# Second attention of a four-layer kernel: values duplicated by GpSimd and q arranged earlier at its beginning; the last network's first two steps moved into its block at its end

## What is computed

```python
x = x + _layernorm(_L0_attn_ref(_layernorm(x), ...))   # linear attention, 16 heads of 128
x = x + _layernorm(_L0_ffn_ref(_layernorm(x), ...))    # 16 experts, top 2, and a shared network
x = x + _layernorm(_L1_attn_ref(_layernorm(x), ...))   # attention in windows of 32 tokens
x = x + _layernorm(_L1_ffn_ref(_layernorm(x), ...))    # SwiGLU network, 1024 wide

def _L1_attn_ref(x, Wq, bq, Wk, bk, Wv, bv, Wo, bo):   # WINDOW 32, 16 heads of 16, 2 groups
    starts = jnp.arange(num_windows) * (W // 2)
    scores = jnp.einsum('brgnqd,bgnkd->brgnqk', qg, kw) * scale
    attn = jax.nn.softmax(scores, axis=-1)
    og = jnp.einsum('brgnqk,bgnkd->brgnqd', attn, vw)
    o = og....reshape(B, num_windows * W, H * D)[:, :L, :]
    return o @ Wo + bo

def _L1_ffn_ref(h_shard, w_gate_up, w_down):
    gate, up = jnp.split(jnp.einsum('bsh,oh->bso', h_shard, w_gate_up), 2, axis=-1)
    h = jax.nn.silu(gate) * up
    return jnp.einsum('bsi,hi->bsh', h, w_down)
```

## Time and profile before

| | us |
|---|---|
| median of 3 runs | 1158.51 (1154.85 to 1162.67) |
| profiled execution, its own time | 1155.04 |
| its span in the trace | 1153.2 |

### The profile page before, as it was taken

How to read it: one execution, slowest core, us unless ns; L and a number is a source line. 1 busy time by engine, 2 the same in 40 slices (tenths; PEclk the granted TensorE clock), 3 DMA queues, 4 the chain that set the end, 5 groups by cost and what they waited for, 6 DMA issues and landing times. The chain is left out here.

```text
span 1153.2 us, 20280 instructions
## 1 busy us (share of the span) xinstructions
PE 1114.8 (97%) x7188; PEld 960.1 (83%) x7188; DVE 743.3 (64%) x1582; ACT 525.1 (46%) x978; POOL 252.7 (22%) x290
## 2 busy tenths in 40 slices
PE   8999999999999999999999999899998889899997
PEld 7997988989989989988988888775555778788897
DVE  6665665665665665665665677755554767686556
ACT  5675344344344344344344354555552466644322
POOL 1112021021021021111111131323332556323211
PEclk9999999999999999999999999799998969999999
DMA  4001001001001001001000000853333324000001
GB/s 156 11 1 37 11 1 38 9 0 36 9 0 36 9 0 36 9 0 36 9 0 1 1 1 4 318 123 97 98 102 96 87 77 147 1 1 1 19 19 38
DMA packets 27979, 48.28 MB, mean 42 GB/s; under 512 B 4780, under 2 KB 18060, under 8 KB 26764
## 3 DMA queue, kind: packets, MB, share of 16 engines
q1 hardware_dynamic: 23980, 37.62, 10.2%
q0 software_dynamic: 3456, 9.44, 3.1%
q10 hardware_dynamic: 480, 0.40, 0.1%
HBM read 35.65 MB, written 9.44 MB: 39 GB/s over the span
## 5 line engine op out<-in xcount | busy, mean ns | idle before, releaser
L880 POOL TENSOR_TENSOR linear_out_row<-linear_out_row,lin_sq 128x512 f32<-128x512 f32 x62 | 89.9, 1450 | 538.3 <-ACT lin_sq L745 536.0
L43 PE MATMUL lin_bank<-keep_xT_hi,lin_w_hi 128*128 128x512 f32 x382 | 154.2, 404 | 0.0
L44 PE MATMUL lin_bank<-keep_xT_lo,lin_w_hi 128*128 128x512 f32 x382 | 151.1, 395 | 0.0
L45 PE MATMUL lin_bank<-keep_xT_hi,lin_w_lo 128*128 128x512 f32 x382 | 150.8, 395 | 0.0
L825 DVE TENSOR_TENSOR lin_st<-lin_bank,lin_mask 128x512 f32<-128x512 f32 x64 | 44.0, 691 | 160.9 <-PE lin_bank L622 160.9
L741 ACT ACTIVATE lin_o<-lin_bank 128x512 f32<-128x512 f32 x64 | 38.3, 599 | 187.7 <-PE lin_bank L653 187.7
L649 PE MATMUL lin_bank<-lin_st,lin_v 128*128 128x128 f32 x512 | 93.8, 275 | 0.0
L653 PE MATMUL lin_bank<-lin_qd,lin_state 128*128 128x128 f32 x448 | 87.2, 276 | 0.0
L45 PEld LDWEIGHTS lin_bank<-keep_xT_hi,lin_w_lo 128*128 128x128 f32 x382 | 71.8, 188 | 17.5
L44 PEld LDWEIGHTS lin_bank<-keep_xT_lo,lin_w_hi 128*128 128x128 f32 x382 | 72.0, 189 | 14.6
L43 PEld LDWEIGHTS lin_bank<-keep_xT_hi,lin_w_hi 128*128 128x128 f32 x382 | 72.0, 188 | 14.6
(11 more groups left out here) (417 smaller groups left out, 2843.2 us busy)
## 6 DMA issues: line engine op xcount, KB each, us to landing
lin_raw<-in_wp SPq DMA_DIRECT2D x7, 1024.0 KB, 4.7
experts_up_expert_up<-in_wgu SPq DMA_DIRECT2D x16, 352.0 KB, 7.3
sorted_y<-shared_loaded SPq DMA_DIRECT2D x40, 128.0 KB, 1.7
linear_out_row<-in_wdn SPq DMA_DIRECT2D x4, 704.0 KB
lin_raw_out<-in_wop SPq DMA_DIRECT2D x8, 256.0 KB, 2.6
tokens_x<-linear_out_row SPq DMA_DIRECT2D x4, 512.0 KB, 10.3
linear_out_row<-in_ffn_up SPq DMA_DIRECT2D x2, 1024.0 KB, 5.8
tail_q<-tail_qT SPq DMA_DIRECT2D x28, 64.0 KB, 2.0
```

The source lines that it names most:

```text
L43: nc.tensor.matmul(out, lh, rh, start=first, stop=False, skip_group_check=skip)
L44: nc.tensor.matmul(out, lh, rl, start=False, stop=False, skip_group_check=skip)
L45: return nc.tensor.matmul(out, ll, rh, start=False, stop=last, skip_group_check=skip)
L880: pool.tensor_tensor(part, part, sq[:, a, :], ALU.add).then_inc(squares_sb, 1)
```

## The change

In `window_attention`, at the beginning: the value copies of batch 0 leave ScalarE; GpSimd makes them (four `tensor_copy`) after its tenth tile has arrived and ahead of b's scale. ScalarE issues half of the q moves of rr = 1 too, and does all four arrangements of batch 0 ahead of the loop (before, one was VectorE's in round 0 and one ScalarE's in round 2). TensorE turns b's tiles in round 2, behind the scores of job 2, instead of round 1.

At the end: `before` and `turn` for segment 0 each move to earlier rounds on GpSimd, VectorE and ScalarE; TensorE's turn goes from round 21 to round 18. Steps 0 and 1 of the last network's `pe_up` are issued in rounds 19 and 21, the split of the up weights of steps 0 to 2 in rounds 11 to 22. The statistics of segment 1 (`before`) move into round 20. In `feed_forward` the steps start with what is left of them, and weights are split three steps ahead, behind a step instead of in front of it. For this the banks, four semaphores, q2, q3 and the up weights are allocated in the scope "window" around both blocks (so `tail_bank` and `ffn_bank` are both called `window_bank`, and `ffn_w_hi` is `window_up_hi`).

```diff
@@ feed_forward
             def _(dve):
                 chain = Chain(dve, own)
                 dve.wait_ge(keep.ffn_ready, 1)
-                net.dve_low(dve, 0)
-                for half in range(2):
-                    before.statistics(dve, chain, 1, half)
-                net.dve_low(dve, 1)
+                net.dve_low_down(dve, 0)
                 for g in range(SEGS):
                     late = LATE if g == 0 else 0
                     for j in range(J):
-                        if g == 0 and j + 2 < J:
-                            net.dve_low(dve, j + 2)
                         net.dve_step(dve, chain, g, j)
+                        if g == 0 and j < 2:
+                            net.dve_low_down(dve, j + 1)
+                        if g == 0 and j + 3 < J:
+                            net.dve_low(dve, j + 3)
...
             def _(act):
                 act.wait_ge(keep.ffn_ready, 1)
-                net.act_high(act, 0)
-                net.act_high(act, 1)
+                net.act_high_down(act, 0)
...
                     for j in range(J):
-                        net.pe_up(pe, g, j)
+                        if g or j >= 2:
+                            net.pe_up(pe, g, j)
...
@@ window_attention, SP and GpSimd
-                        move_q(sp, b, rr, (0, 1) if b == rr == 0 else range(4))
+                        move_q(sp, b, rr, range(4) if b else (0, 1))
...
                     if n == BATCH * USED_TILES:
+                        for t_ahead in ORDER[n - AHEAD:n]:
+                            pool.wait_ge(arrived[t_ahead], 2 * DMA)
+                        pool.wait_ge(kv_sb, 2)
+                        for half in range(2):
+                            v = kvT[GD:2 * GD, 0, half * STEP:half * STEP + WPAIRS * WIN].rearrange("p (m k) -> p m k", k=WIN)
+                            for g in range(WG):
+                                pool.tensor_copy(vdup[GD:2 * GD, :, half, g, :], v).then_inc(vdup_sb, 1)
+                        pool.wait_ge(vdup_sb, 2 * WG)
                         b.pool_scale(pool, chain, "y")
                         b.pool_scale(pool, chain, "x")
...
                     if n == 6:
+                        before.affine.scale_and_shift(pool, chain, 0)
+                    if n == 7:
                         b.pool_shift_x(pool)
...
-                    if n == 7:
-                        before.affine.scale_and_shift(pool, chain, 0)
-                    if n == 11:
+                    if n == 10:
                         turn.affine.scale_and_shift(pool, chain, 0)
@@ window_attention, VectorE
-                    if i == NJ - 1:
+                    if i == NJ - 3:
                         dve.wait_ge(a.shifted, a.n)
                         before.add(dve, 0)
+                    if i == NJ - 2:
                         dve.wait_ge(before.added, 1)
                         for half in range(2):
                             turn.statistics(dve, chain, 0, half)
-                    if i == 0:
-                        arrange(0, 1)
...
-                    if i == NJ + 5:
+                    if i == NJ - 1:
+                        dve.wait_ge(s_mm, NJ)
+                        ffn.dve_low_up(dve, 0)
+                    if i == NJ + 1:
+                        ffn.dve_low_up(dve, 1)
+                    if i == NJ + 3:
                         turn.dve_low(dve, 0)
+                    if i == NJ + 4:
+                        for half in range(2):
+                            before.statistics(dve, chain, 1, half)
+                    if i == NJ + 6:
+                        ffn.dve_low_up(dve, 2)
@@ window_attention, ScalarE
                 take_q(0, 1)
-                duplicate(0)
-                arrange(0, 0)
+                move_q(act, 0, 1, (2, 3))
                 act.wait_ge(powered, 1)
                 act.activation(table[:], power[:, 0:1], ACT.Exp)
+                arrange(0, 0)
                 values(0)
-                arrange(1, 0)
+                for part in range(2):
+                    arrange(1, part)
+                arrange(0, 1)
...
-                    if i == 2:
-                        arrange(1, 1)
...
-                    if i == NB + 5:
+                    if i == NB + 3:
                         before.act_apply(act, 0)
+                    if i == NB + 4:
+                        for n in range(BATCH * RR):
+                            act.wait_ge(q3_sb[n], 2)
+                        ffn.act_high_up(act, 0)
+                    if i in (NB + 5, NB + 6):
+                        ffn.act_high_up(act, i - NB - 4)
...
-                    if i == NJ + 1:
+                    if i == NJ:
                         turn.act_apply(act, 0)
-                turn.act_high(act, 0)
+                    if i == NJ + 2:
+                        turn.act_high(act, 0)
@@ window_attention, TensorE
-                    if i == 1:
+                    if i == 2:
                         pe.wait_ge(used[0].low, KT + 1)
                         used[1].pe_turn(pe, turned)
...
-                    if i == NJ + 5:
+                    if i == NJ + 2:
                         turn.pe_turn(pe, 0)
...
+                    if i == NJ + 3:
+                        pe.wait_ge(less_sb, NJ)
+                        pe.wait_ge(pT_sb, NJ)
+                        pe.wait_ge(turn.low, KT)
+                        ffn.pe_up(pe, 0, 0)
+                    if i == NJ + 5:
+                        ffn.pe_up(pe, 0, 1)
```

84 lines of the change are left out of this document (56 added, 28 removed).

## The result

The changed kernel's median is 1162.49 us (1160.27 to 1173.19, 20 runs), that of the kernel before, run beside it, 1158.42 (1154.85 to 1162.67, 20 runs): a ratio of 1.0054 with an interval of 1.0037 to 1.0071. Forecast were 1157 and a change of -0.1%. The kernel became slower by half a per cent. That is inside the range of 1151 to 1163, and inside the 1% that was called no change.

A forecast was written before the change was run, and what follows sets the result against it. TensorE was taken as the bound, so only its standstills or lower clock matter. Terms -1.2, -1.5 and +1.4 sum to -1.3 us on the profiled 1155.04: 1153.7, or about 1157 as median; range 1151 to 1163.

The forecast's parts named there:

- +1.4 for the end: Segment 1's turn in the last network was to come later by 1.4 us, bounds +0.3 and +3.4.
- -1.3: Sum of all terms in us: -1.2 for job 3's sooner scores, -1.5 for the clock, +1.4 for the end.
- the 3.0 us by which the copies were to hold up VectorE: At the beginning, GpSimd's four copies, served between VectorE's sums of b, were to delay the first subtraction to 930.8.
- the clock's term: Full clock some 4 us earlier than at 945, speeding batch 1's values and projections: -1.5 us, bounds 0 and -3.
- The rival of copies that disturb nobody: At the beginning, copies quick or without disturbance: -3.5 to -4.8 in sum, 1154.5 us; chance 0.24.
- ScalarE's list: Ahead of the loop: DMA issues end at 923.8, arrangements at 931.0; nothing won on ScalarE there.
- 1.2 was summed: At the beginning, job 3's scores at 937.7 instead of 938.88, a gain of 1.2 us.
- The rival that the clock would return only with the projections: At the beginning, scores and turns would not bring full clock back earlier: +0.2 in sum, 1158.7 us; chance 0.20.
- -2.7 of the sum: The whole gain at the beginning: -1.2 for job 3's scores and -1.5 for the clock.
- The gap: At the change of blocks, TensorE waits 2.85 us, as step 2 needs step 0's product; step 2 starts at 1012.4.
- The rival "late turn": In the last block, TensorE stands over 3 us ahead of segment 1's turn, then lower clock: 1160.9 us; chance 0.18.
- The 1.65 us of lower clock at the change of blocks: TensorE's loss to a clock of 0.50 from 1007 to 1010 us, expected again in the changed kernel.

The follow-up runs named there:

- group 4: Runs of start_again, the changed end alone, and batch 1's sooner arrangement with and without the changed beginning; kernel before 1156.74 us, stops in 4 of 4 profiles.
- start_only: The kernel before with the edits of the beginning alone: 1159.53 us, ratio 1.0027 to the kernel before.
- start_again: The kernel before with the beginning of the change alone, run a second time, beside stops: 1159.55 us, ratio 1.0016.
- repeat: The changed kernel again, nothing left out, beside stops: 1160.92 us, ratio 1.0035 to the kernel before.
- groups 1, 4: Kernels run on one chip beside the kernel before, which took 1157.34 and 1156.74 us; ScalarE stops of 6 us or more in 4 of 4 profiles each.
- 2, 3 and 5: The other groups of runs; kernel before 1153.77, 1153.67 and 1154.03 us, with no ScalarE stop of 6 us or more in any profile.
- changed_third: The changed kernel a third time, nothing left out, where nothing stops: 1155.87 us, ratio 1.0010 to the kernel before.
- both: Changed kernel with batch 1's first arrangement behind round 7's subtraction, turn statistics ahead of splits, and ScalarE's `before` norm behind step 1's silu: 1150.66 us, ratio 0.9972.
- before_again: The kernel before, unchanged, run for a second profile, which has no stops: 1154.39 us, ratio 1.0002.
- arrange_b1: The changed kernel with VectorE's first arrangement of batch 1's q directly behind the subtraction of round 7: 1151.13 us, ratio 0.9978 to the kernel before.
- start_third: The kernel before with the beginning of the change alone, a third time, without stops: 1152.14 us, ratio 0.9984.

## Why the prediction was off, step by step

**On record.** Two costs add up to the +0.54%. The change's own are +0.1%: the beginning at 0.9984 and the whole at 1.0010 leave +0.26% or 3.0 us for the end, a difference between two groups, and the traces have 2.6. The rest, 0.4% or some 5 us, appears only beside stops. That stops cost the new beginning more than the old is shown by every profile that has them (the table in group 4). Up to the turn of segment 1 they leave the old beginning 0.8 to 1.4 us later than without them (three profiles), the new one 1.5 to 13.9 (start_only, start_again, repeat and the result's). That they make up the whole of the rest is argued, from groups 1, 4 and the result against 2, 3 and 5. What causes the stops is open: they came in two groups with every kernel, with either form of the beginning, and in the three others with none. The prediction had only one profile of the kernel before and no step for them. The measured 1162.49 lies inside the stated range by luck: its upper end was reckoned for a turn 3.4 us late with a second stretch of lower clock, and what brought the time there were mostly stops.

**Which steps failed.** The sum has nothing for the work behind batch 1's first projections, where 4.5 us of the beginning's gain are lost again, and it takes +1.4 for the end where 2.6 to 2.7 came. Together these turn -1.3 into +1.3. A third step, the 3.0 us by which the copies were to hold up VectorE, failed the other way, and so did the size of the clock's term up to job 8.

**GpSimd's copies: sized within bounds, their effect wrong.** The four copies, GpSimd's, and VectorE beside them in changed_third:

```profile
919.04 3.01 POOL L2572 COPY tail_oP<-linear_out_row 32x512 f32<-32x512 f32 x4 [2.04 <-DMA linear_out_row<-sorted_y,keep_slots]
920.31 0.71 DVE L2623 SCALAR_TENSOR_TENSOR keep_y<-linear_out_row,keep_weight,keep_y 128x256 f32<-128x256 f32 x1
927.94 0.68 DVE L2659 TENSOR_REDUCE tail_most<-window_bank 128x16 f32<-128x512 f32 x1
```

The four take 3.01 us together, 0.75 each from start to start (0.95 taken, 0.45 to 1.45 bounded). The failed step is "If each copy is served between two of them, VectorE is late by ... 3.0". The worst of VectorE's sums beside a copy takes 0.71 instead of 0.48, and the first subtraction begins at 927.94 where the earlier trace rows have 927.78: late by 0.2 and not 3.0 (0.3 counted from batch 0's projection, 0.5 to 0.6 in the other profiles without stops). The Trainium skill's page "SBUF — State Buffer", section "Who interferes with whom", calls the port pair that the two engines share an exclusive lock. The rows agree that they disturb each other: the single copies take from 0.61 to 0.89 us here, and the shortest is the only one with no sum beside it. But VectorE's share of it is 0.23 us at most, and not a whole copy. At GpSimd's add it is nearly the whole of it (below). The rival of copies that disturb nobody was nearly right on this point; its sum, for the record, is -3.7 to -4.8 and not -3.5 to -4.8.

**ScalarE's list: right.** Second issues end forecast at 923.8, the table load began at 923.53. The arrangements were forecast to end at 931.0:

```profile
927.00 3.38 ACT L2755 ACTIVATE window_q<-window_q 64x512 f32<-64x512 f32 x3
930.80 2.06 ACT L2331 ACTIVATE window_turn_z<-keep_x,tail_used_shift_x,tail_used_scale_x 128x256 f32<-128x256 f32 x4
```

They end at 930.38. With VectorE's chain undelayed b's norm starts at 930.80, not 933.2, and job 3's scores at 935.31, not 937.7:

```profile
930.42 2.07 PE L2910 MATMUL window_bank<-linear_out_row,window_q 64*128 64x128 f32 x8 [0.67 <-ACT window_q L2755]
935.31 1.16 PE L2910 MATMUL window_bank<-linear_out_row,window_q 64*128 64x128 f32 x8
938.21 0.37 PE L2857 MATMUL window_bank<-keep_xT_hi,window_wkv_hi 128*128 128x264 f32 x1
```

The gain there is some 3.5 us (25.2 against 21.7 and 21.5 in the table), where 1.2 was summed and 2.1 named for undisturbed engines.

**The clock: sign right, size and end wrong.** Job 3's scores take 1.16 us, at 2.4 GHz, where those of job 2 took 2.07. The level came back between the two, some 10 us before 945, not 4. The rival that the clock would return only with the projections is refuted for this profile: between the scores of job 2 and of job 3 TensorE's timeline has four transposes of probabilities (932.42) and ten of b's turn (933.33 to 935.3), and no projection. It isn't so each time. Of the seven profiles without stops that have this beginning, six have full clock at job 3; in that of both, the same work in the same order, the scores of job 3 take 2.07 us and the clock comes back only in the projections, so that these start 1.8 us later. By the Trainium skill's page "TensorE: Matmul & The Clock Gate", section "Part 4: PE-mode transpose", the full clock does not engage for transposes; here it was back at the end of them, and whether they or the scores ahead of them brought it back the rows don't tell.

Up to job 8 the beginning gains 6.0 us, more than twice the -2.7 of the sum. Then 4.5 of it goes again from job 8 to job 10: 11.5 us against 7.0, with a clock of 0.50 for some 10 us. In before_again the clock falls at the same place, 45 us behind batch 0's projection, but for some 3 us, and all but 0.1 us of it hidden behind VectorE's chain to job 8. The prediction followed the clock up to "projections of batch 1 from 943.35" and put everything behind them at nothing, without a reason: it asked neither what else sets the time between job 7 and job 8, nor what the clock does there. This is the step that was left out. arrange_b1, which takes 1.5 us off VectorE's chain, gets 3.0 of the 4.5 back; why the lower clock lasts three times as long in the changed kernel stays open.

**The end: the gap right, its price under-sized.** The rows on which it turns, in changed_third, of four engines in order of time:

```profile
1009.45 0.69 DVE L1356 TENSOR_TENSOR ffn_h<-ffn_silu,window_bank 128x512 f32<-128x512 f32 x1
1010.43 0.77 PE L1386 MATMUL window_bank<-keep_xT_hi,window_up_hi 128*128 128x512 f32 x1 [2.90 <-ACT window_up_hi L1281]
1013.57 2.42 POOL L1123 TENSOR_TENSOR keep_x<-keep_x,window_before_z 128x1024 f32<-128x1024 f32 x1 [2.19 <-ACT window_before_z L1129]
1014.32 1.96 DVE L1302 TENSOR_TENSOR ffn_d_lo<-linear_out_row,ffn_d_hi 128x256 fp32r<-128x256 f32 x1 [1.99 <-ACT ffn_d_hi L1286]
1025.96 0.74 DVE L1007 BATCH_NORM_STATS2 window_turn_stats<-keep_x 128x6 f32<-128x256 f32 x2
1031.71 1.09 PE L1157 MATMUL window_bank<-keep_ident,window_turn_z 128*128 128x128 f32 x8 [1.83 <-ACT window_turn_z L1129]
```

The gap is 2.90 us (2.85 forecast), step 2 starts 0.3 us behind the product of step 0 (the trace names ScalarE's split, which also ends then, as releaser), as forecast, and the clock is 0.50 behind it. The two steps end at 1007.5, which is 93.95 us after batch 0's projection against 89.36 for the old block's end: 4.6 later, and with the beginning's 1.4 us taken out 6.0, where 6.3 were forecast. The statistics of the second half begin 16.5 us behind VectorE's first product (1009.45), where 15.15 were forecast (1011.75 to 1026.9). The wait for ScalarE is 1.99 us instead of 0.85, which is nearly all of the difference; ScalarE's norm of `before` stands ahead of that split. The price at the turn is 2.6 to 2.7 us. The computed +2.4 was good. The failed step is "Half of the 1.3 and half of the 0.8 may not come; I take +1.4": of the 0.8 some 0.5 came, of the 1.3 all (1.96 us where the other splits of this kind take 0.42), and the wait was longer still. The rival "late turn" named the mechanism and was given 0.18, but its condition did not come: TensorE waits 1.83 us ahead of the turn, not over 3 (nor over 2, as the last paragraph of the prediction has it), and no lower clock follows.

The 1.65 us of lower clock at the change of blocks, which the prediction carried as a loss both kernels have, are worth nothing. In before_again the clock falls there, in start_third it doesn't; first step to turn takes 1030.66 - 1005.58 = 25.08 us in the one and 1026.66 - 1001.58 = 25.08 in the other, since start_third waits 1.27 us for VectorE instead. VectorE's chain sets this part.

**Sum.** By its own terms, measured without stops: beginning -1.4 (-2.7 forecast; it is a gain of 6.0 and a loss of 4.5 that was not foreseen), end +2.7 (+1.4 forecast), together +1.3 (-1.3 forecast). With the two terms wrong in the same direction the sign was wrong, within a tenth of a per cent each.

The version with both edits is faster than the kernel before: 0.9972 and 0.9965 in two groups, 3 to 4 us. Both groups were without stops; beside stops it wasn't measured.
